# First graph attention: logarithms of edge counts added to the exponent, in odd steps by GpSimd and in even steps by VectorE

## What is computed

```python
hh = h.reshape(n, H, D)                      # n = 1250, H = 12, D = 64
ft = einsum('nhd,ed->nhe', hh, W_fc)
a1 = einsum('nhd,hd->nh', ft, attn_l)        # of the source node
a2 = einsum('nhd,hd->nh', ft, attn_r)        # of the destination node
e = leaky_relu(a1[src] + a2[dst], 0.2)
m = segment_max(e, dst)
ee = exp(e - m[dst])
alpha = ee / segment_sum(ee, dst)[dst]
agg = segment_sum(alpha[:, :, None] * ft[src], dst)
```

## Time and profile before

| | us |
|---|---|
| runs: median | 3747.34 |
| runs: lowest, highest | 3734.17, 3749.85 |
| the profiled execution, its own time | 3740.85 |
| its span in the profile | 3738.9 |
| busy: PE, DVE, ACT, POOL | 2830.1, 2123.3, 1267.4, 340.6 |
| mean granted TensorE clock, as a share of full speed | 0.855 |

### The profile page before, as it was taken

One profiled execution on the slowest core, in us unless ns is written; L12 is line 12 of the kernel. 1 busy time (PEld: TensorE's weight loads), 2 busy tenths in 40 slices (PEclk: granted clock), 3 DMA queues, 4 the chain that ended last, 5 costly groups with the idle time before them and its releaser, 6 DMA issues. The chain is left out here.

```text
span 3738.9 us, 37335 instructions
## 1 busy us (share of the span) xinstructions
PE 2830.1 (76%) x12998; PEld 2120.4 (57%) x12999; DVE 2123.3 (57%) x3299; ACT 1267.4 (34%) x1700; POOL 340.6 (9%) x179
## 2 busy tenths in 40 slices
PE   4773695788753575599399997994899669998848
PEld 2442595233242475455299997894788545565623
DVE  4556298999841243497098887620666863124331
ACT  0232221988610010111188885120655510013110
POOL 0000000000023674100000000510000000000010
PEclk9997755999955899699699997797999879999869
DMA  1115152111026743452623322436332511000031
GB/s 49 34 37 201 30 168 86 52 42 42 14 70 186 263 163 111 154 189 82 168 80 97 96 78 69 138 119 148 120 93 89 156 37 51 26 26 1 1 75 41
DMA packets 161517, 343.71 MB, mean 92 GB/s; under 512 B 33036, under 2 KB 85308, under 8 KB 159992
## 3 DMA queue, kind: packets, MB, share of 16 engines
q1 hardware_dynamic: 115280, 222.07, 19.3%
q10 hardware_dynamic: 38576, 100.22, 8.3%
q0 software_dynamic: 7520, 19.53, 1.7%
HBM read 262.63 MB, written 79.10 MB: 91 GB/s over the span
## 5 line engine op out<-in xcount | busy, mean ns | idle before, releaser
L1105 PE MATMUL rg1a_acc<-rg1a_values,rg1a_high 125*125 125x193 f32 x2400 | 404.1, 332 | 74.5 <-DMA rg1a_values<-values_dram 71.1
L1105 PEld LDWEIGHTS rg1a_acc<-rg1a_values,rg1a_high 125*125 125x125 f32 x2400 | 400.1, 191 | 78.6 <-issue 60.9
L1272 PE MATMUL gat_acc<-far_u,gat_ft 125*65 125x512 f32 x720 | 291.9, 549 | 73.6 <-DVE far_u L1336 73.0
L1153 DVE TENSOR_TENSOR rg1a_high<-rg1a_high,rg1a_lowb 125x625 f32<-125x625 f32 x240 | 194.4, 810 | 152.9 <-ACT rg1a_lowb L1129 135.5
L1751 PE MATMUL rg2a_acc<-rg2a_value_part,rg2a_wts_part 125*125 125x512 f32 x600 | 206.1, 343 | 65.5 <-DVE rg2a_wts_part L1511 55.9
L1272 PEld LDWEIGHTS gat_acc<-far_u,gat_ft 125*65 125x65 f32 x720 | 96.4, 145 | 265.3 <-issue 173.8
L901 PE MATMUL rg_out<-rg_w,rg_hT 128*125 128x384 f32 x720 | 232.9, 487 | 0.0
L1128 ACT ACTIVATE rg1a_high<-rg1a_rows,rg_ks 125x625 f32<-125x625 f32 x240 | 196.3, 818 | 101.7 <-DMA rg1a_rows<-rows_dram 45.6
L1752 PE MATMUL rg2a_acc<-rg2a_value_part,rg2a_wts_part 125*125 125x512 f32 x600 | 206.7, 344 | 0.0
L1753 PE MATMUL rg2a_acc<-rg2a_value_part,rg2a_wts_part 125*125 125x512 f32 x600 | 205.1, 342 | 0.0
L1166 DVE SCALAR_TENSOR_TENSOR rg1a_high<-rg1a_high,rg1a_counts 125x625 f32<-125x625 f32 x240 | 193.0, 805 | 0.0
(11 more groups left out here) (426 smaller groups left out, 5488.1 us busy)
## 6 DMA issues: line engine op xcount, KB each, us to landing
rg2a_values<-values_dram SPq DMA_DIRECT2D x90, 384.0 KB
rg1a_values<-values_dram SPq DMA_DIRECT2D x240, 96.0 KB, 1.9
rg_mask<-far_dram SPq DMA_DIRECT2D x60, 312.5 KB, 3.2
moe_raw<-in_L_ffn_w SPq DMA_DIRECT2D x16, 1152.0 KB, 5.9
gat_rows<-rows_dram SPq DMA_DIRECT2D x12, 1250.0 KB, 5.8
rg1a_rows<-rows_dram SPq DMA_DIRECT2D x24, 625.0 KB, 7.2
relw_chunk<-in_L_gnn_W ACTq DMA_DIRECT2D x36, 384.0 KB, 3.1
sorted_dram<-sort_rows SPq DMA_DIRECT2D x30, 384.0 KB, 5.1
```

The source lines that it names most:

```text
L1105: last = pe.matmul(tile_of(u, d), wts[i % HB][:, d * TP:(d + 1) * TP], stream[i % 4][:, :], start=first and d % per_bank == 0, stop=final, ...
L1153: dve.tensor_tensor(high[i % HB][:, 0:w], high[i % HB][:, 0:w], lowb[i % LB][:, 0:w], op=ALU.max).then_inc(max_done, 1)
L1272: last = pe.matmul(acc[h % 2][0:WIDTH, b, 0:c1 - c0], ft[:, t, h, :], wts[i % HB][:, c0:c1], start=(t == 0), stop=(t == NT - 1))
```

## The change

The weight count x exp(e - m) becomes exp(e - m + log count). With e = max(row 0 + a1, row 1 + 0.2 a1) - the two rows have the maximum already subtracted - it is also 0.2 a1 + max(row 0 + 0.8 a1, row 1). So `greatest` makes `ks_gap` = 0.8 a1 as well. In each of the 120 steps VectorE makes `high` = max(row 0 + ks_gap, row 1) by a scalar-tensor-tensor instruction (`lift`, two steps ahead). Then the logarithms of tile t are added to it in place: in even steps by VectorE with a scalar-tensor-tensor instruction (times 1, plus logs), in odd steps by GpSimd with a tensor-tensor instruction. ScalarE makes the weights with one exponential, whose bias is `ks_low`. `larger` and the multiplication with the counts are gone.

Ahead of the loop the ten tiles of logarithms are made: VectorE writes -1e30 where the count is 0 (else 0) and max(count, 1) into two buffers of `high`, ScalarE takes Ln of the second, and the sum of both goes to `logs[t]`, by VectorE for even t and by GpSimd for odd t. Four of the buffers of `high` serve in turn, so tile t waits for the sum of tile t - 2. Five of the `logs` have memory of their own and five are laid over the counts already used.

```diff
--- before.py
+++ after.py
@@ -610,7 +610,7 @@
 def greatest(g, tag, heads, group, row, mask_of, ks, qd, ks_low, shifted, score_of=None, beside=None,
-             junk=None):
+             junk=None, ks_gap=None):
@@ -688,9 +688,11 @@
             act.activation(rowsT[:, 8 * TP:N], turn_ps[:, 2, 0:2 * TP], ACT.Copy).then_inc(copied, 1)
             act.activation(ks_low[:, :, :], ks[:, :, :], ACT.Copy, scale=0.2).then_inc(low_scaled, 1)
+            if ks_gap is not None:
+                act.activation(ks_gap[:, :, :], ks[:, :, :], ACT.Copy, scale=0.8).then_inc(low_scaled, 1)
             if other:
                 other.scalar(act)
-            act.wait_ge(low_scaled, 1)
+            act.wait_ge(low_scaled, 1 if ks_gap is None else 2)
         @block.sync
         def _(sp):
@@ -1206,14 +1208,14 @@
                 pool.memset(stream[i][:, width:width + 1], 1.0).then_inc(ones, 1)
-def attend_narrow(g, tag, ks, ks_low, shifted, ft, res):
-
-
-
-
-
-
-    H = ks.shape[2]
+def attend_narrow(g, tag, ks_gap, ks_low, shifted, ft, res):
+
+
+
+
+
+
+    H = ks_gap.shape[2]
     WIDTH = ft.shape[3]
     DV = WIDTH - 1
     pieces = [(0, 512), (512, 1024), (1024, N)]
@@ -1230,15 +1232,20 @@
         masks = g.far_u[:, :, :].rearrange("p t n -> p (t n)").bitcast(F32)
         high = [masks[:, i * N:(i + 1) * N] for i in range(NT // 2)]
-        lowb = [s.sb(f"{tag}_lowb{i}", [TP, N])[:, :] for i in range(4)]
-        HB, LB = len(high), len(lowb)
+        HB, LEAD = len(high), 2
+        merged = g.counts_u[:, :, :].rearrange("p t n -> p (t n)").bitcast(F32)
+        logs = ([s.sb(f"{tag}_log{i}", [TP, N])[:, :] for i in range(NT // 2)]
+                + [merged[:, i * N:(i + 1) * N] for i in range(NT // 2)])
         sumsT = s.sb(f"{tag}_sumsT", [WIDTH, N])
         recip = s.sb(f"{tag}_recip", [TP, NT])
         acc = [s.ps(f"{tag}_acc{i}", [128, 3, 512]) for i in range(2)]
         back = s.ps(f"{tag}_back", [TP, 2, 512])
         turned, copied, rows_out = s.sem(f"{tag}_turned"), s.sem(f"{tag}_copied"), s.sem(f"{tag}_rows_out")
         rows_in = s.sems(f"{tag}_rows_in", 2)
-        exp_done, max_done, wts_done = s.sem(f"{tag}_exp"), s.sem(f"{tag}_max"), s.sem(f"{tag}_wts_done")
+        lifted, wts_done = s.sem(f"{tag}_lifted"), s.sem(f"{tag}_wts_done")
+        counts_up, log_taken = s.sem(f"{tag}_counts_up"), s.sem(f"{tag}_log_taken")
+        even_logs, odd_logs = s.sem(f"{tag}_even_logs"), s.sem(f"{tag}_odd_logs")
+        even_added, odd_added = s.sem(f"{tag}_even_added"), s.sem(f"{tag}_odd_added")
         multiplied, sums_out, sums_turned = s.sem(f"{tag}_multiplied"), s.sem(f"{tag}_sums_out"), s.sem(f"{tag}_sums_turned")
         taken, v_chain = s.sem(f"{tag}_taken"), s.sem(f"{tag}_vc")
         block = s.block()
@@ -1283,6 +1290,10 @@
                            ACT.Copy).then_inc(copied, 1)
             act.activation(shiftedT[:, 8 * TP:N], acc[1][0:2 * H, 2, 0:2 * TP], ACT.Copy).then_inc(copied, 1)
+            for t in range(NT):
+                act.wait_ge(counts_up, t + 1)
+                act.activation(high[2 * t % 4], high[2 * t % 4], ACT.Ln).then_inc(log_taken, 1)
+
             def copy_sums(h):
                 act.wait_ge(multiplied, (h + 1) * NT)
                 if h >= 1:
@@ -1292,16 +1303,11 @@
                                ACT.Copy).then_inc(sums_out, 1)
             for i, (h, t) in enumerate(steps):
-                if t == 0:
-                    act.wait_ge(rows_in[h % 2], h // 2 * 16 + 16)
-                if i >= HB:
-
-                    act.wait_ge(multiplied, i - HB + 1)
-                if i >= LB:
-                    act.wait_ge(max_done, i - LB + 1)
-                act.activation(high[i % HB], rows[h % 2][:, 0, :], ACT.Exp, bias=ks[:, t, h:h + 1])
-                act.activation(lowb[i % LB], rows[h % 2][:, 1, :], ACT.Exp,
-                               bias=ks_low[:, t, h:h + 1]).then_inc(exp_done, 1)
+                if i % 2 == 0:
+                    act.wait_ge(even_added, i // 2 + 1)
+                else:
+                    act.wait_ge(odd_added, i // 2 + 1)
+                act.activation(wts[i % HB], high[i % HB], ACT.Exp, bias=ks_low[:, t, h:h + 1]).then_inc(wts_done, 1)
                 if t == COPY and h >= 1:
                     copy_sums(h - 1)
             copy_sums(H - 1)
@@ -1310,10 +1316,31 @@
         def _(dve):
             link = chain(dve, v_chain)
-            def larger(i):
-                dve.wait_ge(exp_done, i + 1)
-                dve.tensor_tensor(high[i % HB], high[i % HB], lowb[i % LB],
-                                  op=ALU.max).then_inc(max_done, 1)
+            def lift(i):
+                h, t = steps[i]
+                if t == 0:
+                    dve.wait_ge(rows_in[h % 2], h // 2 * 16 + 16)
+                if i >= HB:
+
+                    dve.wait_ge(multiplied, i - HB + 1)
+                dve.scalar_tensor_tensor(out=high[i % HB], in0=rows[h % 2][:, 0, :], scalar=ks_gap[:, t, h:h + 1],
+                                         in1=rows[h % 2][:, 1, :], op0=ALU.add, op1=ALU.max).then_inc(lifted, 1)
+
+            def add_even_log(t):
+                dve.wait_ge(log_taken, t + 1)
+                dve.tensor_tensor(logs[t], high[2 * t % 4], high[(2 * t + 1) % 4], op=ALU.add).then_inc(even_logs, 1)
+
+            for t in range(NT):
+                if t >= 2 and t % 2 == 0:
+                    dve.wait_ge(even_logs, t // 2)
+                elif t >= 2:
+                    dve.wait_ge(odd_logs, t // 2)
+                dve.tensor_scalar(high[(2 * t + 1) % 4], g.counts_u[:, t, :], 0.5, FAR, op0=ALU.is_lt, op1=ALU.mult)
+                dve.tensor_scalar(high[2 * t % 4], g.counts_u[:, t, :], 1.0, None, op0=ALU.max).then_inc(counts_up, 1)
+                if t % 2 == 1:
+                    add_even_log(t - 1)
+            dve.wait_ge(even_logs, NT // 2)
+            dve.wait_ge(odd_logs, NT // 2)
             def take_out(h):
                 dve.wait_ge(sums_turned, h + 1)
@@ -1328,17 +1355,29 @@
                                                     op0=ALU.mult, op1=ALU.add)
                 last.then_inc(taken, 1)
-            larger(0)
+            for i in range(LEAD):
+                lift(i)
             for i, (h, t) in enumerate(steps):
-                if i + 1 < len(steps):
-                    larger(i + 1)
-                dve.wait_ge(max_done, i + 1)
-                dve.scalar_tensor_tensor(out=wts[i % HB], in0=high[i % HB], scalar=1.0,
-                                         in1=g.counts_u[:, t, :], op0=ALU.min, op1=ALU.mult).then_inc(wts_done, 1)
+                if i + LEAD < len(steps):
+                    lift(i + LEAD)
+                if i % 2 == 0:
+                    dve.wait_ge(lifted, i + 1)
+                    dve.scalar_tensor_tensor(out=high[i % HB], in0=high[i % HB], scalar=1.0, in1=logs[t], op0=ALU.mult,
+                                             op1=ALU.add).then_inc(even_added, 1)
                 if t == TAKE and h >= 1:
                     take_out(h - 1)
             take_out(H - 1)
             dve.wait_ge(taken, H)
+
+        @block.gpsimd
+        def _(pool):
+            for t in range(1, NT, 2):
+                pool.wait_ge(log_taken, t + 1)
+                pool.tensor_tensor(logs[t], high[2 * t % 4], high[(2 * t + 1) % 4], op=ALU.add).then_inc(odd_logs, 1)
+            pool.wait_ge(odd_logs, NT // 2)
+            for i in range(1, len(steps), 2):
+                pool.wait_ge(lifted, i + 1)
+                pool.tensor_tensor(high[i % HB], high[i % HB], logs[steps[i][1]], op=ALU.add).then_inc(odd_added, 1)
         @block.sync
         def _(sp):
@@ -1348,7 +1387,7 @@
             for h in range(H):
                 if h >= 2:
-                    sp.wait_ge(exp_done, (h - 1) * NT)
+                    sp.wait_ge(lifted, (h - 1) * NT)
                 src = bass.AP(tensor=g.rows_dram.tensor, offset=h * N, ap=[[0, P], [H * N, 2], [1, N]])
                 sp.dma_start(rows_all[h % 2][:, :, :], src).then_inc(rows_in[h % 2], 16)
@@ -1564,6 +1603,7 @@
         ks = s.sb("gat_ks", [TP, NT, H])
         qd = s.sb("gat_qd", [TP, NT, H])
         ks_low = s.sb("gat_ks_low", [TP, NT, H])
+        ks_gap = s.sb("gat_ks_gap", [TP, NT, H])
         shifted = s.sb("gat_shifted", [TP, NT, 2, H])
         res = s.sb("gat_res", [TP, NT, D])
         with ExitStack() as inner:
@@ -1578,8 +1618,8 @@
                 sm = Scope(g, inmost)
                 row = [sm.sb(f"gat_row{i}", [P, 1, N])[:, :, :] for i in range(3)]
                 greatest(g, "gat", H, 1, row, None, ks, qd, ks_low, shifted,
-                         beside=lambda sc: RelationWeights(sc, g, layers, weights))
-            attend_narrow(g, "gat2", ks, ks_low, shifted, ft, res)
+                         beside=lambda sc: RelationWeights(sc, g, layers, weights), ks_gap=ks_gap)
+            attend_narrow(g, "gat2", ks_gap, ks_low, shifted, ft, res)
         added = s.sem("gat_added")
         block = s.block()
```

## The result

The changed kernel takes 3806.43 us (median of 4 runs, 3799.06 to 3817.58); the kernel before, with one more run beside them, 3743.36 (4 runs). The ratio is 1.0171 with a 95% interval of 1.0144 to 1.0198: slower, by 63 us where 80 were forecast (3823, range 3790 to 3885). The profiled execution took 3805.98 us, its span is 3804.2.

The account below looks back on a forecast made before the run. VectorE alone was taken to bound the stage. Prelude 24.8, loop and tail 49.8 and clock 5 made 79.6 us more than the profiled 3740.85, 3820; allowing for the runs' median gave 3823, range about 3790 to 3885.

Parts of the forecast that it names:

- Turns: In the loop, GpSimd additions and VectorE's two-input instructions take turns; a pair of steps costs 6.77 us against 5.48 before.
- The hold: In the loop, each GpSimd addition of 2.82 us blocks VectorE for 2.66 us; 60 of them make 159.6 us.
- The lift: VectorE's scalar-tensor-tensor in each step of the loop was put at 1.37 us, like the other two-tensor forms.
- 417.8: Forecast us from the first lift to the stage's end, where 368.0 was before.
- The outputs at nothing: Outputs of eleven heads, 2.37 us each, lie beside GpSimd's addition and cost nothing; up to 26 us if not.
- The prelude, +24.8: Making ten logarithm tiles ahead of the loop puts the first lift at 682.0, 24.8 us later than 657.19.
- The clock, +5: In the loop, TensorE's granted clock sometimes falls to half after gaps of about 2.5 us; 5 us taken.
- The profile: Expected signs in the stage: lifts of 1.46 and about 4.1 us, 6.8 us a pair, first lift at about 682.
- The first, no turns: Rival: scalar-tensor-tensor in the loop does not take turns with GpSimd; 3695 us, between 3680 and 3735; chance 0.11.
- The second, TensorE at half clock throughout: Rival: TensorE's clock settles at half and bounds the loop, some 8.5 us a pair; up to 3930; chance 0.06.
- the third: Rival: partial overlap in the loop, GpSimd's hold shorter than 2.66; at 1.4 the program takes 3765; chance 0.04.

Follow-up runs that it names:

- idle additions: Kernel before, with 60 GpSimd additions of 1250 columns on spare buffers in its loop that nobody waits for: 3880.64 us in one run, stage 522.6.
- memsets: Changed kernel with GpSimd's odd-step additions replaced by memsets of a spare buffer, odd logarithms missing from the weights: 3734.66 us in one run, stage 362.4.
- the run without odd additions: Changed kernel with no GpSimd instruction in the loop, odd logarithms missing from the weights: 3744.03 us in one run, stage 362.3.

## Why the prediction was right

**Turns.** The deciding step was that the scalar-tensor-tensor form would be blocked, although no row of before showed it under a GpSimd instruction. It was: 3.65 to 4.1 us in the changed kernel, up to 4.1 in the kernel before with idle additions, where both forms together got 144 us longer. The Trainium skill, SBUF — State Buffer, section "Who interferes with whom", says that a VectorE instruction with two SBUF inputs contends with a GpSimd instruction that reads SBUF, and that one that only writes does not contend; the traces agree on both (stages of 362.4 with and 362.3 without memsets, the output with a PSUM operand undisturbed at 2.01). Its rule that the later one waits for the whole of the other agrees with the changed kernel, less some 0.2 us. With idle additions, five GpSimd additions waited much longer, one of them through 19 instructions of VectorE. The prediction's "they take turns" was thus right for this kernel and is not so in general.

**The hold, 2.66 forecast.** It was 2.21 in the 24 pairs of t = 1 and 3 and 2.65 in the others (6.44 and 6.88 less 2 x 1.43 + 1.37); eleven of the others lie beside an output. The line through 768 and 2304 columns fitted the slow buffers only. That is 24 x 0.45 = 11 us less than forecast. The lift was put at the 1.37 of the other forms and starts every 1.43: 120 x 0.06 = 7 us more. With these two, 417.8 becomes 414; measured are 415.2 us from the first lift, 0.9 of them the one wait named under the clock (before 368.0).

**The outputs at nothing.** Right: GpSimd's 2.84 lie beside them. The instruction behind the output is 0.02 to 0.49 us longer, so that the output and this lengthening take about the 2.66 us that were put down for the addition's hold.

**The prelude, +24.8.** The first lift comes 36.3 us after the first transpose, where VectorE's first instruction came after 14.5: +21.8. A tensor-scalar starts every 0.72 (I took 0.80), and GpSimd's addition holds 2.2 there too. Tensor-scalars at 0.55 would have been 4 us less, not the 3 that I wrote.

**The clock, +5.** VectorE waited 0.9 us for a matmul in the whole loop (the lift's waits in the stage, in us and times):

```profile
  issue: 2.5, 1
  PE gat_acc L1279: 0.9, 1
```

The granted clock did fall at times (0.86 over 675:775, 0.98 over 875:975, below; before 0.97 and 0.93), but the delay stayed inside the slack of the buffers all but once. The step was right in kind and 4 us too dear.

```profile
675.00:775.00 100.00, 69.45 (x180) 25.77 (x181) 98.38 (x69) 38.11 (x30) 54.44 (x16) 0.86 0.10 31
...
875.00:975.00 100.00, 69.70 (x209) 27.32 (x208) 99.61 (x76) 41.44 (x33) 53.45 (x16) 0.98 0.11 37
```

Sum: 21.8 + 47.2 = 69.0 in the stage, against 79.6. Three terms were each some us too high, the hold most of all; one, the lift, too low. The rest of the miss is 3.6 us of the earlier start of the stage in this execution, and the 3 us that I added because the profiled execution was a fast one. The low end of the range adds up to 3795, not 3790; the measured 3806 lies inside either.

**The profile.** The period of 6.8 us a pair came as 6.44 and 6.88. The long VectorE instructions are not the lifts, as I wrote, but the even additions behind them: with few exceptions the lifts keep their 1.51. The first lift came at 675.3, not 682, 3.6 us of that by the earlier start.

**The rivals.** The first, no turns, would have won less than I wrote: the run without odd additions puts its stage at 362, some 3720, not 3695; TensorE's gap behind the outputs, with its half clock, was missing in its working. The second, TensorE at half clock throughout, did not come: the granted clock was 0.50 over 675:685, 0.72 over 685:695, where TensorE was busy all the time, and 1.00 over 695:705. Nor did the third, which needed a hold of about 1.4: measured were 2.2 and 2.65.

## What to carry to other kernels

An engine with nothing to do is no free resource if its reads of SBUF and those of the engine that is the bound exclude each other: here each addition moved to GpSimd saved VectorE 1.37 us and cost it 2.2 to 2.65. Look in the trace for the places where the two engines already met, and take the period of the turns, not the mean length, as the price. What GpSimd can take over is work that falls beside instructions of VectorE with an operand in PSUM, or work that only writes; one such instruction per head won 0.4% in the kernel before, while the sixty of the changed kernel, eleven of them covered, cost its stage 42.5 us against VectorE doing all itself. In the changed kernel one instruction per head won next to nothing (408.1 against 408.9), since the lift then waited for its buffer. And the change would have lost without GpSimd too: 3766 against 3739, by its prelude above all.

## What the runs showed of the hardware

GpSimd's in-place constant addition over 1250 float columns takes 3.38 us, longer than its addition of two tensors (2.40 or 2.83). The latter has these two lengths in the loop by the buffer that it works on in place; moving the second operand changed neither. A per-partition scalar read from SBUF lengthens VectorE's scalar-tensor-tensor instruction from 1449 to 1509 ns. A single-input tensor-scalar of VectorE from 16 bits to float (0.80 us) is blocked by a GpSimd addition just like the two-input forms (2.89 to 3.02). A GpSimd addition can be kept waiting through 19 back-to-back two-input instructions of VectorE (28.61 us from its start to its end in the kernel with idle additions).
